# Routing in a four-layer graph kernel: row fetches and row scatters on 128 partitions where there were 126

## The reference, cut to what matters

```
h = leaky_relu(x @ weight + bias).reshape(N, 8, 16)
h_normed = h / |h|                        # per capsule
h_dst = h_normed
for _ in range(4):
    scores = sum(h_dst[row] * h_normed[col])          # per edge and capsule
    alpha  = softmax of scores over the edges of one row
    agg    = segment_sum(h_normed[col] * alpha, row)
    node_attr = agg + h_normed
    h_dst = node_attr / |node_attr|
```

## Time and profile before

| | us |
|---|---|
| median of 3 runs | 5265.04 (5263.86 to 5271.49) |
| the profiled execution, its own time | 5274.68 |
| its span, first to last instruction | 5272.9 |
| PE / DVE / POOL / ACT busy | 3360.3 / 3707.9 / 2918.3 / 2381.2 |

### The profile page before, as it was taken

How to read it: one execution, slowest core, us unless ns; L and a number is a source line. 1 busy time by engine, 2 the same in 40 slices (tenths; PEclk the granted TensorE clock), 3 DMA queues, 4 the chain that set the end, 5 groups by cost and what they waited for, 6 DMA issues and landing times. The chain is left out here.

```text
span 5272.9 us, 70797 instructions
## 1 busy us (share of the span) xinstructions
PE 3360.3 (64%) x20489; PEld 2676.9 (51%) x20592; DVE 3707.9 (70%) x10180; ACT 2381.2 (45%) x5571; POOL 2918.3 (55%) x2733
## 2 busy tenths in 40 slices
PE   6888855277612377653166653555999993875664
PEld 1455544277601255543166652333777772775663
DVE  8877777299834476632277767886888883775887
ACT  6444400199800165532123222553666662333887
POOL 2577577345577433247777745774777655304700
PEclk9999987599955599975588876887999997998887
DMA  5666688299857778742267635884555553886874
GB/s 219 182 187 194 174 309 291 76 298 318 252 183 262 244 261 280 245 138 80 74 196 259 206 92 166 280 281 148 172 185 186 183 174 109 259 252 204 278 247 168
DMA packets 684357, 1095.96 MB, mean 208 GB/s; under 512 B 108888, under 2 KB 451979, under 8 KB 677722
## 3 DMA queue, kind: packets, MB, share of 16 engines
q1 hardware_dynamic: 580772, 908.27, 52.9%
q0 software_dynamic: 103200, 183.16, 11.6%
HBM read 664.33 MB, written 439.19 MB: 209 GB/s over the span
## 5 line engine op out<-in xcount | busy, mean ns | idle before, releaser
L2240 PE MATMUL ro_end<-vals,end_mask 128*2 128x128 f32 x1600 | 236.9, 312 | 378.9 <-DVE vals L2104 275.6
L2366 POOL DMA_INDIRECT sc_rows<-layer,node_idx x400 | 391.5, 979 | 124.4 <-issue 121.6
L719 POOL DMA_INDIRECT agg<-late_agg_sent,d_last x200 | 218.1, 1091 | 324.9 <-issue 299.0
L2240 PEld LDWEIGHTS ro_end<-vals,end_mask 128*2 128x2 f32 x1600 | 146.1, 95 | 461.4 <-DVE vals L2104 286.7
L2972 ACT ACTIVATE tf_hidden<-tf_h_ps,pre_b 128x512 f32<-128x512 f32 x392 | 268.8, 687 | 227.3 <-PE tf_h_ps L3012 216.8
L2266 PE MATMUL ro_acc<-vals,ro_mask 128*126 128x128 f32 x1600 | 245.4, 318 | 187.2 <-ACT ro_square L2198 140.4
L3024 PE MATMUL tf_o_ps<-pre_w,tf_hidden 128*128 128x128 f32 (+1 forms) x3136 | 358.1, 275 | 0.0
L1599 POOL DMA_INDIRECT cap_own<-layer,w_own x200 | 205.0, 1025 | 273.9 <-SPq L1579 221.1
L3024 PEld LDWEIGHTS tf_o_ps<-pre_w,tf_hidden 128*128 128x128 f32 (+1 forms) x3136 | 353.9, 192 | 0.5 <-issue 0.5
L3012 PE MATMUL tf_h_ps<-tf_x_t,pre_w 128*128 128x512 f32 x784 | 348.2, 597 | 9.4 <-ACT tf_hidden L2972 8.2
L2054 POOL TENSOR_TENSOR vals<-ro_both,ro_weight 126x1024 f32<-126x1024 f32 x75 | 144.9, 1932 | 342.2 <-ACT ro_weight L2222 252.3
(11 more groups left out here) (493 smaller groups left out, 10984.9 us busy)
## 6 DMA issues: line engine op xcount, KB each, us to landing
ro_mask<-masks SPq DMA_DIRECT2D x100, 504.0 KB, 4.7
layer<-zeros SPq DMA_DIRECT2D x96, 512.0 KB
si_both<-layer SPq DMA_DIRECT2D x48, 1024.0 KB, 6.0
ro_far<-far SPq DMA_DIRECT2D x75, 512.0 KB, 6.2
ro_both<-both SPq DMA_DIRECT2D x75, 512.0 KB, 6.0
agg<-zeros SPq DMA_DIRECT2D x48, 512.0 KB
mom_x<-in_x_dram SPq DMA_DIRECT2D x48, 512.0 KB, 8.8
mom_agg<-agg SPq DMA_DIRECT2D x48, 512.0 KB, 7.5
```

The source lines that it names most:

```text
L719: pool.indirect_dma_start(out=self.dest, out_offset=bass.IndirectOffsetOnAxis(ap=self.order.last_idx[:, t:t + 1], axis=0), in_=self.sent[: ...
L2240: mm = nc.tensor.matmul(end_ps[0:2, j, :], k.end_mask[:, t, :], k.vals[:, t, :], start=True, stop=True, skip_group_check=True)
L2366: nc.gpsimd.indirect_dma_start(out=rows[:, g % SC, c * GT + j, :], out_offset=None, in_=k.layer1, in_offset=bass.IndirectOffsetOnAxis(ap=k ...
```

## The change

The three kinds of indirect DMA of the routing take all 128 partitions. The data path around them (what is stored into `own_rows`, what DVE computes, what PE sums) is as before. For the two rows more, `wide.own` has the rows of the tile's first and last id; `wide.far` has row number 1 (twice the zero id, plus one); and two new small copies on DVE put the first and the last id into the "next" row too, so that own id and next id are equal there, and `wide.last` gets a number beyond the table: these rows of a scatter are left out.

```diff
 capsules_phase, fetch
-                            out=own[0:RE, g % SC, j, :], out_offset=None, in_=k.layer1_halves,
-                            in_offset=bass.IndirectOffsetOnAxis(ap=wide.own[0:RE, t:t + 1], axis=0))\
+                            out=own[:, g % SC, j, :], out_offset=None, in_=k.layer1_halves,
+                            in_offset=bass.IndirectOffsetOnAxis(ap=wide.own[:, t:t + 1], axis=0))\
 wide_order_phase
                 v.tensor_copy(row3[:, :, 1, 0:RE], row4[:, :, :, 1])
+                v.tensor_copy(row3[:, :, 2, RE:RE + 1], row4[:, :, 0:1, 0])
+                v.tensor_copy(row3[:, :, 2, RE + 1:RE + 2], row4[:, :, RE - 1:RE, 0])
 routing_phase, gather
-                            out=far[real, u, j, :], out_offset=None, in_=k.layer1_halves,
-                            in_offset=bass.IndirectOffsetOnAxis(ap=wide.far[real, t:t + 1], axis=0))\
+                            out=far[:, u, j, :], out_offset=None, in_=k.layer1_halves,
+                            in_offset=bass.IndirectOffsetOnAxis(ap=wide.far[:, t:t + 1], axis=0))\
 routing_phase, scatter
-                            out=k.layer1_halves, out_offset=bass.IndirectOffsetOnAxis(ap=wide.last[real, t:t + 1], axis=0),
-                            in_=sent[real, u, j, :], in_offset=None, bounds_check=2 * N - 1, oob_is_err=False)\
+                            out=k.layer1_halves, out_offset=bass.IndirectOffsetOnAxis(ap=wide.last[:, t:t + 1], axis=0),
+                            in_=sent[:, u, j, :], in_offset=None, bounds_check=2 * N - 1, oob_is_err=False)\
```

## The result

The changed kernel took 5250.14 us (median of 7 runs, 5239.04 to 5258.03), the kernel before in the same series 5268.93 (5263.86 to 5292.98): ratio 0.9966, interval 0.995 to 0.9981, or 18.8 us between the medians. Run twice more, with 12 runs each, it came to 0.9979 (0.9968 to 0.999) and 0.9981 (0.9965 to 0.9998). So the effect is clear, and its size is more likely some 10 to 14 us than 19. My forecast was -2.4 us with a range from 5253 to 5271 and 0.83 for no change; the sign was right, the size and the range were not.

A forecast was written before the change was run, and what follows sets the result against it. Bounds: capsule work then POOL's tail for own rows, SP's queue loop for far rows, POOL for final scatters. Terms +0.3 - 0.7 - 0.6 - 0.6 - 0.8 = -2.4 us took 5265.0 to 5262.6 us; range 5253 to 5271.

The forecast's parts named there:

- Fetches, 35 ns each: Own and far row fetches each cost POOL 35 ns less, mostly hidden: -0.7 us own rows, -0.6 us far rows.
- rival 1: POOL, not SP's queue, paces the first step, so fetch savings there count: -6.4 us more, 5256 us; chance 0.08.
- the loop over SP's queue: First step: DVE, SP's end sums, then own-row loads set the pace at 11.77 us a unit; POOL needs 11.3.
- Two copies: Two added DVE copies in the order phase, on DVE's path: +0.3 us, bounds 0.1 and 0.4.
- Last step: Final scatters: POOL never stands still and is the limit, 200 x (1.071 + 0.30) = 274 us.
- 200 x 3 ns: Final scatters: the 128-partition form costs POOL 3 ns less each, -0.6 us; bounds -7 and +3.1.
- Earlier landing: Final scatters: fewer packets land 0.05 us sooner, shortening stalls beside DVE in about 16 units: -0.8 us, bounds 0 and -2.4.
- Rivals 2 to 4: Last-step stalls vanish, 5246 us (0.06); more first-step stalls, 5277 (0.08); two extra rows cost what they save, 5265.3 (0.09).

The follow-up runs named there:

- c1: The kernel before run again without any edit; ratio 0.9995 (0.9983 to 1.0006).
- c3: The kernel before plus only the two small id copies on DVE, no DMA changed; ratio 0.9998 (0.9987 to 1.0009).
- c2: The changed kernel run again without a further edit; ratio 0.9979 to the kernel before.
- f1: The changed kernel run a third time without a further edit; ratio 0.9981 (0.9965 to 0.9998) to the kernel before.
- d2: The kernel before with the first step's end sums written out one unit later in SP's queue; ratio 0.9979 (0.9962 to 0.9996).
- d3: The changed kernel with the first step's end sums one unit later in SP's queue; ratio 0.9956 (0.9939 to 0.9973) to the kernel before.

## Why the prediction was wrong, step by step

Where the time went, from the starts of the first POOL instruction of each stage in three profiles each (kernel before, c1, c3 against after, c2, f1):

| stage | without, us | changed, us | difference of means |
|---|---|---|---|
| first layer, to first payload scatter | 681.2, 679.5, 673.8 | 677.7, 679.3, 695.2 | +5.9, 17 us of f1's long fetch in it |
| payload scatters, to first own fetch | 398.0, 395.8, 397.6 | 393.9, 396.1, 392.7 | -2.9 |
| capsules | 417.1, 417.4, 417.3 | 417.3, 416.3, 415.5 | -0.9 |
| first step | 345.8, 344.3, 345.6 | 342.6, 345.2, 344.2 | -1.2 |
| steps 2 and 3 | 472.0, 471.3, 470.1 | 475.2, 476.8, 466.7 | +1.8, not told apart |
| last step | 277.7, 278.4, 280.4 | 274.7, 274.8, 274.5 | -4.2 |
| scores | 613.9, 614.3, 613.6 | 614.5, 612.3, 611.0 | -1.3 |
| third layer, messages (L791) | 623.7, 624.3, 623.2 | 624.5, 625.1, 621.7 | 0.0 |
| third layer, edges (L2873) | 639.2, 638.5, 642.3 | 640.8, 640.8, 642.7 | +1.5 |
| last layer | 804.3, 799.7, 800.7 | 793.4, 794.0, 797.4 | -6.6 |

The rows add up to -8 us, the difference of the mean spans (5267.0 and 5259.0 us). Six stages are shorter by 17 us together; the others give 9 back, and most of that is the one long fetch of f1.

Two steps of the prediction failed: it let lines outside the change keep their time, and it took 3 ns for the change of form of a scatter. Part by part:

- **Fetches, 35 ns each:** right (40 and 35 measured), and so was that capsules and first step hide nearly all of it: -0.7 and -0.6 were forecast, -0.9 and -1.2 measured, within the spread. (In the first profile alone the first step is 3.2 us shorter, which would have spoken for rival 1; c2 and f1 do not repeat it.) d2 and d3 confirm the loop over SP's queue as the pace that hid them, which rival 1 denied.
- **Two copies:** +0.3 us forecast, 0.14 in the timeline, since the copies overlap. Within the bounds, and too little to matter.
- **Last step:** POOL's own pace, right. The term "200 x 3 ns" failed: I took the price of a 128-row scatter from L719 of the old program, 982 ns, and in the new program this very line has 972 to 975. The scatter fell by 11 to 13 ns, 2.2 to 2.6 us where 0.6 was forecast. My bounds of +3.1 to -7 held it.
- **Earlier landing:** mechanism and sign right. In the steady units at the end of the step DVE starts 0.11 us earlier after a scatter than before (1.40 against 1.51 us from the end of the scatter that it waits for), and 17.4 us of stalls became 16.5. Over the three profiles each, stalls fell by 1.6 us (from 17.4, 18.0 and 19.8 to 16.5, 17.1 and 16.8), where 0.8 was forecast. With the 2.6 us of the medians that is the whole -4.2, against -1.4 forecast.
- **"Unchanged lines keep their time":** this unspoken step failed: the sum put them at nothing without a reason. Every term of my sum stood in the four changed places. Payload scatters, 200 at 9 to 12 ns less in a stage where POOL never stops, give -1.8 to -2.4 us of the -2.9 measured.
- **Last layer:** -6.6 in the means, of the stage where 200 of the cheaper scatters (L719) run; their own 2 us do not cover it. Own fetches alone (e1) had 793.8 there with scatters at 982, and far with scatters (e4) had 803.5 at 972. Over all 18 profiles, the twelve with these scatters at 982 or 983 have 793.3 to 806.2 us, mean 799.8, and the six with 972 to 974 have 793.4 to 803.5, mean 797.1. So the spread between programs is larger than the effect, the -6.6 may in part be chance, and a cause beyond the scatters' own 2 us is not shown.
- **Rivals 2 to 4:** none came. The last step keeps 16.5 us of stalls, the first step is not longer, and the fetches have medians of 944 to 947 ns.
- **Range and chances:** I took the spread from three runs, 7.6 us. Single executions of the kernel before spread over 25 to 47 us in the later series, those of the changed kernel over 19 to 34. The two later ratios, on the first series' 5268.93, would give some 5258 us, inside my range; the sum would have been off even so, with -2.4 us for some -10.

What stays open: why the time of an unchanged scatter depends on the form of another line. It repeats within 3 ns for each program, it shows in scatters that run ahead of the changed ones, one form among 200 is not enough, and two extra instructions on DVE do not cause it. I did not vary anything else of the program's layout.

The Trainium skill (DMA: Bandwidth & Descriptors, section on why a DMA increments its semaphore by 16) says that the number of engines is the largest up to 16 that divides the rows, with 127 partitions on a single one. The runs with 112, 126, 127 and 128 rows agree with it, for indirect DMAs from POOL: 14 packets of 4096 bytes for a fetch of 126 rows, and 127 rows in 16 packets with 32-byte ones beside them. In POOL's time it was 38 ns for 14 engines in place of 16 and 1.59 us for one in place of 16. I had used the rule only for transfer lengths, where it changed nothing.

## What to carry to other kernels

Give an indirect DMA a number of rows that is a multiple of 16 even if some rows are waste: of the four sizes tried here 112 and 128 were cheaper than 126, and 127 cost 9% of the whole program. Before counting such a saving, look for the loop that paces the stage, and expect stalls beside DVE to eat part of what POOL gains once POOL is the pace. And when a change of 0.1% is forecast, take the spread from many executions, repeat the old kernel's profile before reading a difference of stages, and add up all stages, also those that got longer.

## What the hardware showed that I had not expected

- A fetch of 127 rows holds POOL for 2538 ns, one of 128 for 944, and makes 272 packets in place of 32.
- Scatters of unchanged lines move by some 10 ns, the same within 3 ns in each profile of one program, with the form of other DMAs.
- With POOL as the pace, 35 ns less per fetch gave nothing (290.8 against 291.5 us): mean 1151 and 1154 ns, as stalls grew.
- In seven of 18 profiles one fetch of the first layer lasts 52 to 89 us, until DVE leaves a loop at about 147 us.
